# Three edits to the hand-written order of a two-layer decoder: fewer empty steps in two attentions, fewer filler matmuls, a table load moved

## What is computed

```
x = x + L0_attn(norm(x))    # "attn0": self attention, 16 heads of 8
x = x + L0_xattn(norm(x))   # "cross0": 8 heads of 64 over 512 context tokens
x = x + L0_ffn(norm(x))     # "mixer": masked attention, 16 heads of 8
x = x + L1_attn(norm(x))    # delta rule, a scan over tokens, gated
x = x + L1_xattn(norm(x))   # "cross1": 16 heads of 64 over 512 context tokens
x = x + L1_ffn(norm(x))     # ternary weights: matmul, Gelu, norm, matmul
# a cross attention:
sim  = einsum('bihd,bjhd->bhij', q, k) * SCALE
attn = softmax(sim, axis=-1)
out  = einsum('bhij,bjhd->bihd', attn, v).reshape(...) @ Wout + bout
```

## Time and profile before

| | |
|---|---|
| time, median of 3 runs | 418.48 us (418.44 to 419.53) |
| the profiled execution: its own time | 419.58 us |
| its span | 417.8 us |
| PE busy, share of the span | 357.5 us, 86% |
| DVE busy | 268.6 us, 64% |
| ACT busy | 210.2 us, 50% |
| POOL busy | 120.3 us, 29% |

### The profile page before, as it was taken

One profiled execution on the slowest core, in us unless ns is written; L12 is line 12 of the kernel. 1 busy time (PEld: TensorE's weight loads), 2 busy tenths in 40 slices (PEclk: granted clock), 3 DMA queues, 4 the chain that ended last, 5 costly groups with the idle time before them and its releaser, 6 DMA issues. The chain is left out here.

```text
span 417.8 us, 7484 instructions
## 1 busy us (share of the span) xinstructions
PE 357.5 (86%) x2813; PEld 205.2 (49%) x2813; DVE 268.6 (64%) x591; ACT 210.2 (50%) x371; POOL 120.3 (29%) x113
## 2 busy tenths in 40 slices
PE   7677689798988989788798997877878999899986
PEld 3443344344554644454465665344444556455555
DVE  6855643666546576776644677969986483867345
ACT  3365467455535454346547543534555663555544
POOL 4000000146454017000000321214866635447500
PEclk9999999999999999999999999999999999999999
DMA  7800000010000000000010000000000000000000
GB/s 194 223 2 1 2 1 2 0 52 2 0 2 2 0 2 1 0 4 1 2 48 6 2 0 2 0 0 2 1 2 2 2 0 2 2 0 3 1 2 25
DMA packets 9688, 6.16 MB, mean 15 GB/s; under 512 B 3755, under 2 KB 8758, under 8 KB 9654
## 3 DMA queue, kind: packets, MB, share of 16 engines
q1 hardware_dynamic: 9654, 5.69, 5.3%
HBM read 5.39 MB, written 0.26 MB: 14 GB/s over the span
## 5 line engine op out<-in xcount | busy, mean ns | idle before, releaser
L1274 DVE TENSOR_REDUCE mxw<-PS 128x2 f32<-128x1024 f32 x48 | 58.5, 1221 | 23.3 <-PE PS L641 23.0
L1045 ACT ACTIVATE Pc<-PS 128x1024 f32<-128x1024 f32 x48 | 49.1, 1022 | 22.5 <-PE PS L669 21.3
L556 POOL TENSOR_TENSOR Psum<-Pc 128x512 f32<-128x512 f32 x24 | 31.0, 1291 | 96.6 <-ACT Pc L1045 95.8
L1271 DVE TENSOR_REDUCE mx<-PS 128x4 f32<-128x1024 f32 x32 | 39.0, 1224 | 21.2 <-PE PS L634 21.2
L697 PE MATMUL ACC<-Pc,V 128*64 128x256 f32 x384 | 52.0, 392 | 0.0
L558 POOL TENSOR_TENSOR Psum<-Psum,Pc 128x512 f32<-128x512 f32 x22 | 27.9, 1267 | 38.6 <-ACT Pc L1045 38.2
L1045 ACT ACTIVATE Ps<-PS 128x1024 f32<-128x1024 f32 x32 | 32.7, 1021 | 11.4 <-PE PS L653 10.6
L697 PEld LDWEIGHTS ACC<-Pc,V 128*64 128x64 f32 x384 | 23.4, 136 | 23.6 <-issue 15.2
L709 PE MATMUL PS<-ones_h 128*128 128x512 f16 x114 | 29.4, 404 | 1.9 <-POOL ones_h L527 1.0
L559 POOL TENSOR_TENSOR Psum<-Psum,Pc 128x512 f32<-128x512 f32 x22 | 28.0, 1272 | 1.7
L662 PE MATMUL PS<-Qhl,Khl_a 64*128 64x256 f16 x384 | 26.5, 271 | 1.0 <-DVE scratch L1444 0.5
(11 more groups left out here) (288 smaller groups left out, 683.5 us busy)
## 6 DMA issues: line engine op xcount, KB each, us to landing
Qm<-mrow SPq DMA_DIRECT2D x64, 0.5 KB, 1.7
wq_c<-in_c_Wq_dram SPq DMA_DIRECT2D x1, 512.0 KB, 5.8
spread<-in_c_Wo_dram SPq DMA_DIRECT2D x1, 512.0 KB
Pc<-in_ctx_dram SPq DMA_DIRECT2D x1, 384.0 KB, 4.8
wk_c<-in_c_Wk_dram SPq DMA_DIRECT2D x1, 384.0 KB, 6.7
wv_c<-in_c_Wv_dram SPq DMA_DIRECT2D x1, 384.0 KB, 8.1
csth<-in_const_dram SPq DMA_DIRECT2D x1, 320.0 KB, 5.2
x<-in_x_dram SPq DMA_DIRECT2D x2, 128.0 KB, 2.3
```

The costliest lines, as they stand in the source:

```text
L556: alone(v.tensor_tensor(t, p[:, :, 0, :], p[:, :, 1, :], ALU.add), "sums_done")
L1045: e = A(to, src.rearrange("p a c -> p (a c)"), ACT.Exp, scale=PHASES[name].scale)
L1271: last = v.tensor_reduce(to, src.rearrange("p e (t s) -> p e t s", t=2), AX, ALU.max)
L1274: last = v.tensor_reduce(to, src, AX, ALU.max)
```

## The change

The change has four edits. In the first call of `attentions`, both parts of cross0 get `late` 1 in place of 2. In the last call, the second sequence of cross1 gets `late` 0 in place of 2. Of the constant products, `dt` of the second sequence has 4 in place of 12 and each `ff2` none (it stood for the first of them only, with 4). The load of the table of Ln and Exp is issued right behind the last Gelu, ahead of three copies that stood before it.

```diff
-    one = attentions((a0, 0, -9, 0), (a0, 1, -3, 0), (x0, 0, 14, 2), (x0, 1, 22, 2))
+    one = attentions((a0, 0, -9, 0), (a0, 1, -3, 0), (x0, 0, 14, 1), (x0, 1, 22, 1))
...
-    three = attentions((y1, 0, -9, 0), (y1, 1, 13, 2))
+    three = attentions((y1, 0, -9, 0), (y1, 1, 13, 0))
...
-    job("dt", "", 1): 12, job("sp", "", 1, 1): 5,
-    job("xt", "", 1, 5): 8, job("fT", "", 1): 3, job("ff2"): 4,
+    job("dt", "", 1): 4, job("sp", "", 1, 1): 5,
+    job("xt", "", 1, 5): 8, job("fT", "", 1): 3,
...
                     A(hb[b][:, i, :], src[:, 0, :], ACT.Gelu).then_inc(freed(j), 1)
+                    if b == 1 and i == 1:
+                        nc.scalar.preload_act_table_set(LN_EXP)
                 elif kind == "fT":
...
                 elif kind == "fr":
-                    nc.scalar.preload_act_table_set(LN_EXP)
                     act.wait_ge(sem("h_var"), 2)
```

## The result

The changed kernel takes 414.79 us in the median of seven runs (412.71 to 416.45). The kernel before took 419.53 in the median of seven runs beside it (418.44 to 419.65). The ratio is 0.9888, with an interval of 0.9866 to 0.9911: 1.1% faster, by 4.7 us. The prediction said 412.8, with a range from 409.8 to 416.0, and it counted from a kernel before at 418.48.

What follows compares the result with a forecast made beforehand. The prediction took PE, busy for 86% of the span, and its waits as the bound. Cross0 4.0, cross1 -0.3, `dt` 1.7 and the end 0.3 sum to 5.7 us, from 418.48 to 412.8, range 409.8 to 416.0.

Steps and rivals of the forecast that it cites:

- Cross0, 4.0 gained: Cross0 with `late` 1: PE's idle time ahead of turns falls from 7.6 us to 3.4-3.8 of waits; bounds 1.5 and 5.5.
- the S behind the Exp of the first unit: Cross0's first unit: S 1 waits for banks until the Exp of S 0 is done, about 0.6 us.
- the new wait at L669: At S 0 in cross0 and cross1, L669 waits for ACT's copy into `negm`: about 0.25 us, some 13 times.
- Cross1, 0.3 lost: Cross1's second sequence with `late` 0: 2.7 us of waits become 3.05; bounds 1.5 gained and 3 lost.
- Rival (e): Cross1's new loop closes at 6.9 us, not 5.57; seven units lose 1.3 each, kernel slower at 425.8; 5%.
- The constants ahead of `dt`, 1.7 gained: Eight constants fewer at 0.216 us each let `dt`'s transposes and all behind them start 1.7 us earlier; lower bound 0.
- rival (b): The clock falls where the constants were, behind 268 us, costing up to 1.7 us: 414.5; 10%.
- its last sign of being wrong: The prediction is wrong if PEclk falls below 1.00 behind 268 us.
- The end, 0.3 gained: Behind the last Gelu, the table load ahead of three copies takes up ACT's idle 0.32 us; Ln starts 0.3 earlier.
- the nine small operations behind Ln: At the end, a chain covering `ff2`'s delay by later copies; without it up to 0.6 us would come back.
- rival (c): At the end, the table load drains ACT first, about 1.38 us by the skill's rule: 414.2; 3%.
- The sum: Whole kernel: 4.0 - 0.3 + 1.7 + 0.3 = 5.7 us gained, from the median of 418.48 to 412.8.

Runs made afterwards that it cites:

- the exchange on ACT: Changed kernel with the copy into `negm` ahead of den's Ln and Exp on ACT in 14 units of cross0 and cross1: 414.27 us, ratio 0.9867.
- the kernel with `dt` back: Changed kernel with the twelve constant products ahead of `dt` of sequence 1 put back: 415.52 us, ratio 0.9904.

## Why the prediction was right, and by how much it was off

**Cross0, 4.0 gained: 3.75.** The mechanism was right: the period, the place of the turn's wait (7.6 to 0.8) and its return with `late` 2 are shown. The first turn's 0.6 stayed, the S behind the Exp of the first unit cost 0.6 as forecast, and the new wait at L669 is 0.20 to 0.25 long and comes 13 times, six of them here. Four of the six cost their whole length, two nothing, so they took 0.98 of the 1.8 that the sum gave them. What the sum didn't have is PE's wait of 0.7 for layer norm's tokens, because DVE's scaling ran slowly there. The two misses are of opposite sign, so some luck is in the 3.75.

**Cross1, 0.3 lost: 0.15 lost.** Both waits traded as said, the 1.1 at the seam against seven of 0.25. The period has a flaw that the number hides. The forecast took 5.57 us for a unit without a Q, from one distance of the kernel before. The distance ahead of that one was 5.22, with this turn as its start:

```profile
373.98 0.44 PE L613 MATMUL PS<-cst,mxw 128*128 128x128 f32 x2
```

In the changed kernel the first of the two is 5.47, which is 5.22 and the wait at L669. The second is 5.57 again, since M 1 waits there for the maxima anyway and hides the wait at S, as the prediction said of that unit. So six of the seven waits cost about 0.25, and one nothing, and that is the size of the miss. That 5.5 came out in cross0, where 5.57 was forecast, is partly luck: it is 5.22 to 5.28 and a wait. Rival (e), the loop that doesn't close, is out: turns of this stage without a Q between them came at most 5.57 apart.

**The constants ahead of `dt`, 1.7 gained: 1.73** in the trace. But rival (b) holds beside it. The forecast gave it 10% and up to 1.7, and its last sign of being wrong, PEclk below 1.00 behind 268 us, came true. The changed kernel's profile shows a fall behind the place: from turn (0,1) to turn (0,2) it takes 6.63 us there (276.89 to 283.52), 5.69 before, so the fall costs 0.94. Over many runs the kernels with four constants have a mean clock lower by 0.005. Of the 1.73 about 0.7 is left between medians of the changed kernels, and 0.8 where the edit was made alone. This is the step that failed: that the clock stays at 1.00 behind the four constants, and that a fall would be an alternative to the gain. It is a tax that some runs pay more often than others. Why eight constants fewer raise it is shown by these averages only; no profile ties one fall to them.

**The end, 0.3 gained: 0.45**, and all of it is the load's. The forecast counted ACT's idle 0.32 and not the 0.14 by which the copies got shorter in one piece. The four constants ahead of `ff2` were free: the nine small operations behind Ln that the prediction named as cover were cover enough with the constants too. The load's row is 1.28 at either place, next to its neighbours. Behind it stands what the Trainium skill says in "ScalarE: Activation LUTs", section "What ACT_TABLE_LOAD costs", of a drain of about 1.38 us with each switch: rival (c), which hung on it, didn't come, and the trace shows no such time on either side of the load.

**The sum.** 5.7 was forecast. At equal clock it is 5.6 to 6.0 (412.71 against 418.30 to 418.72 at 1.000) and 5.5 to 5.8 (413.90 against 419.35 to 419.74 at 0.996), with one run of the changed kernel at each; the trace without its fall at 279 gives 4.8 + 0.94. The medians gained 4.7. The measured 414.79 is 2.0 above the forecast 412.8. About 1.0 of it is the base: three runs had given 418.48, and the seven gave 419.53. The other 1.0 is the lower clock of the changed kernel. By its ratio the forecast (0.9864) lies just outside the measured interval.

## What to carry to other kernels

Compare runs at equal granted clock, and starts in two traces, before believing or doubting a term of a microsecond: here the terms of cross0 and of `dt` and the sum agreed with the trace to about 0.4 in that way, while the medians showed 0.7 of a term of 1.73 and gave that of the load the wrong sign. Constant products ahead of a late instruction cost their whole time on the path, but they also held the clock for what follows; the same products placed inside another wait cost nothing. With them there the median hardly moved in the changed kernel (414.56), and went from 414.27 to 412.5 and 412.33 together with the exchange on ACT, so it is worth trying, and not sure. When a step is taken out of a software pipeline, look which short copy now stands behind a pair of other work on its engine, and put it first: that was worth 2.15 us of the two stages here, more than half of what the step itself gave.

## What the runs showed of the hardware

The clock's falls are not tied to a place. In the profiles of these kernels they came at 20, 37, 51, 160, 167, 249, 267, 279, 281, 307 and 309 us, one to three in an execution (the one at the end left out), each down to 0.50, mostly behind a stretch in which PE had waited for a microsecond or more in one piece. One came where it had not waited at all for 2 us: in the kernel with `dt` back, the windows (PE busy 2.00 of 2 us, then the fall)

```profile
158.00:160.00 2.00, 2.00 (x11) 1.21 (x12) 0.00 (x0) 0.99 (x1) 1.82 (x3) 1.00 0.00 0
160.00:162.00 2.00, 2.00 (x5) 0.72 (x4) 1.69 (x4) 0.81 (x2) 1.17 (x1) 0.59 0.00 0
```

Runs of one kernel without any fall exist as well (mean clock 1.000). What decides in an execution where it falls stays open.

Two of DVE's operations that read no PSUM ran slowly beside POOL's additions. The scaling of layer norm (`xn`, 128x128) took 1256 to 1431 ns in all four cases of cross0 in the changed kernel, each time with such an addition under way, where the median of 24 before was 346 ns and only the slowest took 1254. Norm's last operation, with two operands in SBUF, takes 424 ns at best and 716 in the median of cross1 in the changed kernel; with the exchange on ACT, which moves it 0.3 us later behind the turn, the median is 426. That it is the shift against POOL's additions is read from the traces, not tested. Norm's first two operations, which read the accumulator in PSUM, take 0.41 and 0.42 beside the same additions. The Trainium skill, "SBUF — State Buffer", section "Who interferes with whom", has a pair of ports between VectorE and GpSimd that one of them holds for a whole instruction; by that rule, the trace agrees, since the 1.26 to 1.43 are more than the 0.34 of the operation alone and less than that and one whole addition of POOL (1.27, together 1.61).
